# Order of maxima units and projections on TensorE in a causal attention pair

## The reference

```python
keys    = einsum('bse,neh->bsnh', residual, W_key)    + Bias_key      # 16 heads of 64
queries = einsum('bse,neh->bsnh', residual, W_query)  + Bias_query
values  = einsum('bse,neh->bsnh', residual, W_values) + Bias_values
scores  = einsum('bknh,bqnh->bnqk', keys, queries) / sqrt(64)
scores  = where(q_idx < k_idx, 1e-10, scores)                         # masked, not minus infinity
out     = einsum('bqnh,nhe->bqe', einsum('bnqk,bknh->bqnh', softmax(scores, 3), values), W_output) + Bias_output
```

## Time and profile before

| | |
|---|---|
| median of three runs | 2272.51 us (2267.11 to 2275.48) |
| the profiled execution | 2269.63 us, span 2267.8 us |
| TensorE matmul busy | 1984.8 us (88%) |
| VectorE busy | 1444.2 us (64%) |
| ScalarE busy | 971.0 us (43%) |
| GpSimd busy | 572.7 us (25%) |
| chain that ended last | TensorE 61%, VectorE 16%, issue 11%, ScalarE 6% |

### The profile page before, as it was taken

The page is one execution under the profiler, slowest core; times in us unless marked ns, Lnnn a source line. Parts: engine busy times, 40 slices in busy tenths (PEclk is TensorE's granted clock), DMA queues, the critical chain, the costliest instruction groups (busy, mean ns, idle before and its releaser), DMA issues.

```text
span 2267.8 us, 31835 instructions
## 1 busy us (share of the span) xinstructions
PE 1984.8 (88%) x10080; PEld 1175.0 (52%) x10080; DVE 1444.2 (64%) x2432; ACT 971.0 (43%) x1358; POOL 572.7 (25%) x543
## 2 busy tenths in 40 slices
PE   6899999996996999997768999999969889999975
PEld 3444444443783555556544444444448755555554
DVE  5678777866417776852366787778662377776432
ACT  2445444441224566551234444444413156656411
POOL 0000000000001687884120000000000037797931
PEclk7899999998887999997969999999979879999977
DMA  2366666678000000000514666666760000000015
GB/s 92 80 142 147 143 148 143 143 163 237 21 1 10 1 10 6 1 1 29 159 33 102 144 148 146 154 151 151 167 203 1 1 10 10 2 6 1 1 61 148
DMA packets 84846, 187.99 MB, mean 83 GB/s; under 512 B 17697, under 2 KB 46754, under 8 KB 83106
## 3 DMA queue, kind: packets, MB, share of 16 engines
q1 hardware_dynamic: 83650, 183.76, 32.3%
q0 software_dynamic: 1024, 2.10, 0.3%
HBM read 178.47 MB, written 8.91 MB: 83 GB/s over the span
## 4 chain that ended last, share of the span: by engine, by line
PE 61%; DVE 16%; issue 11%; ACT 6%; DMA 3%; SPq 1%; POOL 1%; DVEq 0%; ACTq 0%; POOLq 0%
PE PS L794 9%; PE PS L766 5%; PE PS L730 5%; PE PS L905 3%; PE PS L945 3%; PE PS L965 3%; DVE mx L1837 3%; PE PS L751 3%; PE PS L756 3%; PE PS L1136 3%; PE PS L948 2%; PE PS L860 2%; PE PS L1191 2%; DMA V<-weight_rows 2%; DVE mrow L1971 2%
## 5 line engine op out<-in xcount | busy, mean ns | idle before, releaser
L1837 DVE TENSOR_REDUCE mx<-PS 128x8 f32<-128x512 f32 x512 | 330.5, 685 | 181.8 <-PE PS L730 170.4
L2337 POOL TENSOR_TENSOR Esum<-Esum,EE 128x512 f32<-128x512 f32 (+3 forms) x320 | 337.5, 1084 | 16.5 <-POOL Esum L2337 10.1
L1866 DVE TENSOR_TENSOR EE<-EE,V 128x1024 f32<-128x1024 f32 x256 | 302.8, 1218 | 45.9 <-DMA V<-weight_rows 45.5
L1457 ACT ACTIVATE EE<-PS 128x1024 f32<-128x1024 f32 x256 | 260.3, 1025 | 143.3 <-PE PS L756 141.4
L2291 POOL TENSOR_TENSOR U<-xn,norm_aff 128x1024 f32<-128x1024 f32 x2 | 4.7, 2356 | 1084.0 <-DVE QA L2262 1084.0
L794 PE MATMUL PS<-EE,Vlater 128*64 128x512 f32 x1024 | 251.9, 611 | 9.1 <-ACT U L1423 8.3
L1971 DVE TENSOR_REDUCE mrow<-PS 128x1 f32<-128x512 f32 (+3 forms) x384 | 203.0, 551 | 86.7 <-PE PS L908 67.4
L730 PE MATMUL PS<-KA,QA 128*128 128x512 f32 x512 | 204.6, 451 | 33.9 <-DVE mx L1837 24.4
L751 PE MATMUL PS<-QA,KA 128*128 128x512 f32 x512 | 184.9, 442 | 0.0
L1541 ACT ACTIVATE EE<-PS 128x1024 f32<-128x1024 f32 (+2 forms) x192 | 137.8, 738 | 105.8 <-PE PS L948 103.8
L730 PEld LDWEIGHTS PS<-KA,QA 128*128 128x128 f32 x512 | 97.3, 195 | 132.8 <-DVE mx L1837 88.5
(11 more groups left out here) (306 smaller groups left out, 3310.3 us busy)
## 6 DMA issues: line engine op xcount, KB each, us to landing
V<-weight_rows SPq DMA_DIRECT2D x512, 256.0 KB, 5.5
EE<-in_w SPq DMA_DIRECT2D x48, 192.0 KB, 2.7
V<-in_Wg SPq DMA_DIRECT2D x4, 1024.0 KB, 6.3
EE<-in_Wu SPq DMA_DIRECT2D x4, 1024.0 KB, 11.4
EE<-in_Wd SPq DMA_DIRECT2D x4, 1024.0 KB, 13.4
sorted_out<-U SPq DMA_DIRECT2D x12, 256.0 KB, 3.1
wo<-in_wo SPq DMA_DIRECT2D x5, 512.0 KB, 3.9
wq_s<-in_wq SPq DMA_DIRECT2D x17, 128.0 KB, 2.9
```

The lines of the kernel that those rows point to most:

```text
L1457: act.activation(EE[i % 2][:, t, :], banks(2 * (t % 2)), ACT.Exp, scale=QSCALE).then_inc(s["p2_exp"], 1)
L1837: dve.tensor_reduce(mx[:, t, half * 8:half * 8 + 8], banks(5 + x % 2, BANK).rearrange("p (c k) -> p c k", c=8), AX, ALU.max).then_inc(s["p ...
L1866: dve.tensor_tensor(EE[i % 2][:, t, :], EE[i % 2][:, t, :], weight_ring[a % 2][:, odd, :], ALU.mult).then_inc(p3_mul, 1)
L2337: ins = pool.tensor_tensor(Esum[:, h, lo:hi], Esum[:, h, lo:hi], e_tile(t)[:, h, lo - t * P:hi - t * P], ALU.add)
```

## The change

In `pair` of `attention1` on TensorE, the two half calls of `project_v` become one call of all four tiles, and K and Q of `project_qk(p + 2, 0)` are issued by one call. The six units 12, 13, 16, 17, 18 and 19, which stood singly between and around these calls, stand in twos: 12 and 13 ahead of `project_v`, 16 and 17 ahead of `project_qk`, 18 and 19 behind `values(p, 2)`. Unit 18 had stood ahead of it.

```diff
                     scores(p, 4, 1)
+                    next_maxima(12, 14)
                     if second:
                         pe.wait_ge(s["p2_exp"], 2 * NT * n + NT)
-                        project_v(p // 2 + 1, p % 2, (0, 1))
-                    next_maxima(12, 13)
-                    if second:
-                        project_v(p // 2 + 1, p % 2, (2, 3))
-                    next_maxima(13, 14)
+                        project_v(p // 2 + 1, p % 2)
                     values(p, 1)
                     next_maxima(14, 15)
                     scores(p, 5, 0)
                     next_maxima(15, 16)
                     scores(p, 5, 1)
-                    next_maxima(16, 17)
+                    next_maxima(16, 18)
                     if second:
                         pe.wait_ge(s["v_out"], 1 + 2 * (g0 + 1) + p + 1)
-                        project_qk(p + 2, 0, "k")
-                    next_maxima(17, 18)
-                    if second:
-                        project_qk(p + 2, 0, "q")
-                    next_maxima(18, 19)
+                        project_qk(p + 2, 0)
                     values(p, 2)
-                    next_maxima(19, 20)
+                    next_maxima(18, 20)
                     values_masked(p)
                     next_maxima(20, 21)
```

## The result

The changed kernel takes 2316.84 us as a median of four executions (2315.09 to 2323.19), the kernel before 2272.59 us beside it (2267.11 to 2275.48). The ratio is 1.0203 with a 95% interval of 1.0175 to 1.023, so +44 us. The direction was forecast, the size was not: +23 us and at most 2307 us were. The profiled execution took 2323.19 us, 53.6 us more than the profiled one of before. Of this, 49.8 us lie in the 14 pairs (556.2 us before, 606.0 us after, summed from one turning of the maxima to the next), 3.8 us in the rest of the program.

The account below looks back on a forecast made before the run. TensorE was taken to hold up VectorE until unit 16, VectorE alone to set the pace from unit 17. Terms 18.4 + 3.2 + 3.0 - 1.4 gave +23.2 us, a median of 2296 us, range 2282 to 2307 us.

Parts of the forecast that it names:

- VectorE's copies: VectorE's diagonal copies at their new times: unknown, -6 to +5 us over 12 pairs, taken as nothing.
- Part one: Units 12 and 13 ahead of the values' projection: TensorE +0.82 us from values(p, 1) on, unit 16 equally later.
- Part two: Units 16 and 17 ahead of K and Q: set at zero, at most 0.3 us without unit 18's lateness as cover.
- Part three: Unit 18 behind values(p, 2): its reduction 2.3 us later in typical pairs, with unit 18's price taken as 0.38 us.
- pair 3 was taken too low: Pair 3, where unit 12 hardly waits: 0.1 us plus 1.5 us, so 1.6 us, twice 3.2 us.
- pair 6's gain: Pair 6, without projections: unit 18 no longer waits behind values(p, 2), gaining 0.7 us, twice 1.4 us.
- Pair 0 was to lose 1.5 us: Pair 0, same pattern as pair 3: unit 18's reduction at 758.31 against 756.79, 1.5 us, twice 3.0 us.
- rival E: New TensorE gaps lower the granted clock for a tenth of each pair: 0.8 us a pair, 10 us on top, 2306 us; chance 0.05.
- A: TensorE's lateness goes through VectorE to m_top in full: +23 us, 2296 us as a median; chance 0.72.
- B: VectorE's copy at 787.11 falls short as in pair 3; typical pairs lose 0.8 us: +11 us, 2284 us; chance 0.11.
- C: Unseen slack of 2.3 us in each pair takes up the stall; only pair 6 changes, 2271 us; chance 0.09.
- D: Blocks bring units earlier without making TensorE late, so VectorE's waits go: -12 us, 2260.5 us; chance 0.03.

Follow-up runs that it names:

- the second gap is filled: Changed kernel plus two extra K projections where TensorE idles ahead of unit 22: ratio 1.0113 to the kernel before, +21 us; pairs +29.0 us.
- both gaps filled: Changed kernel plus four extra values' projection matmuls ahead of unit 12 and three K projections ahead of unit 22: ratio 1.014; with two K projections 1.0101.
- The filling of the first gap: Changed kernel plus four extra values' projection matmuls where TensorE idles ahead of unit 12: ratio 1.0155 to the kernel before, +33 us; pairs +28.3 us.
- the first part alone: Kernel before with only units 12 and 13 moved ahead of an undivided project_v: ratio 1.0054, +11 us; pairs +12.7 us.
- the same move: ScalarE's second_k moved behind exponents(p, 4, 1): in the kernel before ratio 0.9939; in the changed kernel 1.005 to the kernel before.

## Why the prediction was right in direction and wrong in size

**The reading of the bound was right.** VectorE sets the pace from unit 17 on, and what is late there comes out at the pair's end, but for what VectorE's copies take or give back by their new times. The kernel with unit 17 alone moved (no change) and the one with unit 18 moved (+15.3 us of pairs) show it from both sides.

**Part one, forecast +0.82 us to unit 16**, measured 0.86 us, but 1.2 us at the pair's end when it stands alone, by VectorE's copies. **Part two, forecast zero**, measured zero. **Part three, forecast 2.3 us for unit 18 in all**, measured 2.6 us, as unit 18's price was 0.10 us and not 0.38. A typical pair was to take 42.5 us and takes 42.5 or 42.6 us in the changed kernel where the clock is 0.98, 42.4 or 42.5 us where the second gap is filled and the clock is 1.00.

The sum of lateness over pairs 1 to 6 was 18.4 + 3.2 - 1.4 = 20.2 us; with both gaps filled it measures 23.0 us at full clock. Of these, the eight typical pairs are 18.5 us, the two pairs 3 are 7.2 us and the two pairs 6 are -2.6 us. The filling of the first gap itself makes pair 3 longer; with the second gap alone filled, pair 3 takes 41.9 us instead of 39.4 us at a clock of 1.00, +2.5 us, which gives 18.5 + 5.0 - 2.6 = 21 us as an estimate of the lateness without filling. That this is within 1 us of the forecast is in part luck: pair 3 was taken too low (1.6 us), because VectorE's copies of tiles 4 and 6 took 1.19 and 1.00 us there instead of 0.56 us each, and pair 6's gain too low as well (0.7 us; it was 1.3 us at a clock of 1.00). VectorE's copies remained the term that can't be told ahead: the one of tile 6 took from 0.44 us (pair 3 with K and Q in a block) to 1.60 us (pair 3 with the first gap filled).

In the changed kernel itself pair 6 gained nothing. It took 39.0 and 41.1 us in the first profile and 38.8 and 38.6 us in the second, instead of 37.1, at a clock of 0.92 to 0.96. Pair 0 was to lose 1.5 us. It took 41.5 and 41.4 us, against 41.3 and 39.7 us before, at low clocks in both kernels, so it says little.

**The step that failed is the granted clock.** The sum held every stretch of TensorE at the speed of the rows before, and the clock was only rival E, at a chance of 0.05 and a price of 0.8 us a pair, worked out from pair 0 and set on top of the sum. Both numbers were wrong. The pairs' +47.7 us in the first profile and +38.4 us in the second are 21 to 23 us of lateness, and the rest, an estimate of 15 to 27 us, is the clock. I had written that the change opens two more gaps of about 1 us, and then let the row speak against it, since the clock was 1.00 with gaps of 0.92 us. That row shows one level of idle time that the clock bears, not that more of it is borne as well. Pair 0 was also the wrong gauge. Its mean of 0.83 is about a third of the pair at the lower level and not the tenth that I had assumed, and it compares one pair with another, which differ in work (174 and 204 matmuls), while the price of a fall is read from like instructions at both levels, 3.52 against 1.89 us for eight projection matmuls. The range ended at 2307 us because E was put on top of A with that small price.

**The rivals.** B (the copy ahead of units 10 and 11 falls short) happened in none of the eight typical pairs of either profile of the changed kernel, where that copy took 1.30 to 1.33 us. C (slack) and D (blocks bring units early) did not: there is no slack, and VectorE's wait for unit 12 is the same 0.40 us. The rule of the Trainium skill (Perfetto Trace Analysis, Matmul Optimizations) that matmuls should run back to back was weighed as an argument for blocks. By that rule the kernel with both gaps filled should be faster than the changed one, and the trace agrees, 1.00 in its pairs and 42.4 us instead of up to 45.5. What the runs show is that of two orders with the same matmuls the one with larger idle stretches has the lower granted clock (0.91 to 0.98 in pairs 1 to 6, where it was 1.00 before), and that joining calls of one kind isn't what decides: K and Q in one block, with unit 18 left ahead of `values(p, 2)`, changed nothing.

**What stays open.** Why the same idle times end in a fall in one pair and not in the next was not settled. The kernel before has the first gap already, in pair 6 of both batches, with 0.93 us idle ahead of `scores(p, 4, 0)` and then this, and its clock is 1.00 there:

```profile
988.66 0.50 PE L905 MATMUL PS<-KA,QA 128*128 128x512 f32 x1 [0.83 <-DVE mrow L1971]
```

In the kernel with the first part alone, the eight typical pairs have their projections behind such a wait, and in one of them the clock fell (3.45 us for the projections). With either gap filled no pair 1 to 5 took more than 43.3 us, where the changed kernel has pairs of 45 us. But that it takes both gaps in one pair is not shown: the second batch's pair 1 took 45.1 us with `values(p, 3)` at 1.30 us, as the fall behind its first gap was longer (3.62 us for the projections, 2.52 us for `values(p, 1)` instead of 1.72). That the superfluous matmuls act only by keeping TensorE busy is the simplest reading, since they change no unit's order, but the first filling also delays units 12 and 13 in pair 3 by 0.5 to 0.6 us. Nor was it found why the granted clock ahead of the first pair 0 is 0.88 in one execution and 0.81 in another.

## What to carry to other kernels

Where a second engine sets the pace and the first feeds it one buffer at a time, independent work belongs between the feeds. Moved behind them, it turns into idle time ahead of a feed and lateness behind it, and both can be worked out from starts and ends in the timeline. When TensorE gains idle time, count a fall of its clock as a term of its own and price it from like instructions at both levels. And look for the existing wait first: moving 2 us of another engine's work off the way made the kernel faster, and no order of the projections that was tried here did.

## What the runs showed of the hardware

Superfluous matmuls in idle stretches made a kernel faster: with four K projection matmuls more in each of 12 pairs, and the units in the same order, the median was 2292.67 us beside 2313.95 us of the changed kernel, timed together. Idle time taken away can be worth more than its length: the same move gave 15.9 us of pairs at a clock of 1.00, and 35 to 44 us where the clock was falling. The granted clock's falls came in other pairs in a second profile of the same program.
